# Three tiles in turn for the decay factors and three for the states of the selective scans

## The reference, cut to what matters

```
def step(h, inp):
    u_t, d_t, B_t, C_t = inp
    dA = jnp.exp(d_t[..., None] * A)
    h = dA * h + (d_t * u_t)[..., None] * B_t[:, None, :]
    y = jnp.einsum('bdn,bn->bd', h, C_t)
    return (h, y)
```

## Time and profile before

| | |
|---|---|
| median of 3 runs | 951.99 us (950.78 to 953.58) |
| span of the profiled execution, first to last instruction | 951.3 us |
| DVE busy | 798.0 us, 84% |
| PE busy | 771.3 us, 81% |
| ACT busy | 552.9 us, 58% |
| POOL busy | 513.2 us, 54% |

### The profile page before, as it was taken

The page is one execution under the profiler, slowest core; times in us unless marked ns, Lnnn a source line. Parts: engine busy times, 40 slices in busy tenths (PEclk is TensorE's granted clock), DMA queues, the critical chain, the costliest instruction groups (busy, mean ns, idle before and its releaser), DMA issues. The chain is left out here.

```text
span 951.3 us, 10709 instructions
## 1 busy us (share of the span) xinstructions
PE 771.3 (81%) x3950; PEld 512.7 (54%) x3950; DVE 798.0 (84%) x671; ACT 552.9 (58%) x953; POOL 513.2 (54%) x240
## 2 busy tenths in 40 slices
PE   3999998987666778688799899898766677877895
PEld 2444443444366667678655444344435566866773
DVE  5899886269899898999989978725889999999983
ACT  3664332126758898889477433212484779888932
POOL 2005995020478697778410299901126969867841
PEclk8899999999899899999899999989998999999998
DMA  3000000000535345355200200000033445545521
GB/s 108 1 0 0 0 0 1 0 1 0 166 111 177 130 179 185 127 178 178 67 1 0 67 1 0 0 0 1 1 99 110 156 156 177 190 144 177 160 86 22
DMA packets 33296, 75.03 MB, mean 79 GB/s; under 512 B 15708, under 2 KB 15844, under 8 KB 33248
## 3 DMA queue, kind: packets, MB, share of 16 engines
q1 hardware_dynamic: 31840, 73.09, 23.2%
q0 software_dynamic: 320, 1.05, 0.5%
q10 hardware_dynamic: 1088, 0.26, 0.1%
HBM read 70.71 MB, written 2.62 MB: 77 GB/s over the span
## 5 line engine op out<-in xcount | busy, mean ns | idle before, releaser
L370 POOL TENSOR_TENSOR arena<-arena 128x1024 f32<-128x1024 f32 x127 | 300.7, 2381 | 92.7 <-DVE arena L1705 81.8
L1705 DVE TENSOR_TENSOR_SCAN arena<-arena,ps 128x1024 f32<-128x1024 f32 x128 | 289.4, 2280 | 19.2 <-ACT arena L931 11.4
L931 ACT ACTIVATE arena<-arena 128x128 f32<-128x128 f32 (+3 forms) x408 | 152.4, 448 | 86.2 <-DVE arena L1632 75.3
L931 ACT ACTIVATE arena<-arena,Amat 128x1024 f32<-128x1024 f32 x128 | 146.0, 1145 | 61.1 <-DVE arena L1705 60.4
L618 PE MATMUL ps<-mat,arena 128*128 128x128 f32 x1016 | 136.4, 279 | 3.3 <-POOL arena L370 2.5
L577 PE MATMUL ps<-mat,arena 128*128 128x128 f32 x560 | 79.1, 287 | 73.3 <-DVE arena L1705 58.6
L618 PEld LDWEIGHTS ps<-mat,arena 128*128 128x128 f32 x1016 | 119.0, 145 | 6.0 <-POOL arena L370 3.7
L577 PEld LDWEIGHTS ps<-mat,arena 128*128 128x128 f32 x560 | 63.3, 142 | 90.6 <-DVE arena L1705 74.2
L737 PE MATMUL ps<-arena,mat 128*128 128x512 f32 x240 | 106.3, 592 | 0.0
L931 ACT ACTIVATE arena<-ps 128x1024 f32<-128x1024 f32 (+2 forms) x65 | 56.1, 873 | 82.5 <-PE ps L449 23.6
L480 PE MATMUL ps<-arena,diag 128*128 128x512 f32 x180 | 83.0, 618 | 2.4 <-DVE ps L1543 2.4
(11 more groups left out here) (205 smaller groups left out, 1291.6 us busy)
## 6 DMA issues: line engine op xcount, KB each, us to landing
arena<-c_rows SPq DMA_DIRECT2D x128, 512.0 KB, 4.0
out<-arena SPq DMA_DIRECT2D x28, 64.0 KB, 2.3
xres<-x POOLq DMA_DIRECT2D x4, 256.0 KB, 5.5
xres<-x SPq DMA_DIRECT2D x4, 256.0 KB, 4.1
arena<-arena SPq DMA_DIRECT2D x4, 252.0 KB
convw<-conv_w SPq DMA_DIRECT2D x1, 576.0 KB
c_rows<-ROWS SPq DMA_DIRECT2D x4, 128.0 KB, 1.9
mat<-mats SPq DMA_DIRECT2D x1, 448.0 KB, 3.9
```

Source lines behind the costliest of these rows:

```text
L370: tt(HC[s % 2], HS[s % 2], CB[s % 4], ALU.mult).then_inc(S("hc"), 1)
L931: return nc.scalar.activation(out_, in_, func, bias=bias, scale=scale, accum_out=accum_out)
L1705: nc.vector.tensor_tensor_scan(HS[q], DA[q], PS[q][:, :], 0.0, ALU.mult, ALU.add).then_inc(S("scan"), 1)
```

## The change

The decay factors take three tiles in turn and so do the states; the waits move out by one scan accordingly. The third `DA` tile is laid over the second half of `BCS` and all of `BT` in the second arena, columns that `TB` partly held; `TB` of that arena moves to the first half of `BCS`. The third `HS` tile is a tensor of its own, 4 KB a partition. `PS` and `HC` keep two tiles, `CB` four, and no stream changes its order.

```
-            d["TB"] = d["BCS"][:, L // 2:L]
+            d["TB"] = d["BCS"][:, 0:L // 2] if k else d["BCS"][:, L // 2:L]
+            at = sum(n for _, n in later[:6])
+            d["DA2"] = arena[:, at + L // 2:at + L // 2 + L]
...
-        DA, HS = [[D[0][f"W{2 * m + q}"] for q in range(2)] for m in (0, 2)]
+        DA = [D[0]["W0"], D[0]["W1"], D[1]["DA2"]]
+        HS = [D[0]["W4"], D[0]["W5"], sb("HS2", L)[:, :]]
...
-                tt(HC[s % 2], HS[s % 2], CB[s % 4], ALU.mult).then_inc(S("hc"), 1)
+                tt(HC[s % 2], HS[s % 3], CB[s % 4], ALU.mult).then_inc(S("hc"), 1)
...
-                    j, q = s // D_STATE, s % 2
+                    j, q = s // D_STATE, s % 3
...
-                    if s >= 2:
-                        act.wait_ge(S("scan"), SCANS * h + s - 1)
+                    if s >= 3:
+                        act.wait_ge(S("scan"), SCANS * h + s - 2)
...
-                if s >= 2:
-                    dve.wait_ge(S("hc"), SCANS * h + s - 1)
-                nc.vector.tensor_tensor_scan(HS[q], DA[q], PS[q][:, :], 0.0, ALU.mult, ALU.add).then_inc(S("scan"), 1)
+                if s >= 3:
+                    dve.wait_ge(S("hc"), SCANS * h + s - 2)
+                nc.vector.tensor_tensor_scan(HS[s % 3], DA[s % 3], PS[q][:, :], 0.0, ALU.mult, ALU.add).then_inc(S("scan"), 1)
...
-                tt(half(HC[1], n), half(HS[1], n), half(CB[3], n), ALU.mult).then_inc(S("end_hc"), 1)
+                tt(half(HC[1], n), half(HS[(SCANS - 1) % 3], n), half(CB[3], n), ALU.mult).then_inc(S("end_hc"), 1)
```

## The result

The changed kernel takes 944.7 us in the median of 4 runs (944.05 to 944.92), the kernel before 952.8 us beside it; the ratio is 0.9925 with a 95% interval from 0.9906 to 0.9944. Forecast were 945.4 us (940.5 to 950.5) and faster with a chance of 0.72. The ratio is not the quotient of these two medians, which is 0.9915 and lies in the interval. A second set of runs of the change gave 0.9929 [0.9912, 0.9946].

The account below looks back on a forecast made before the run. DVE was taken to set the pace in both scan stretches, with 15.8 us of waits at scans. Gains of 3.70 us (first half) and 2.92 (second) made 6.6, so 952.0 - 6.6 = 945.4 us, range 940.5 to 950.5.

Parts of the forecast that it names:

- Scans 11, 16, 17: First half: waits put on ACT; 2.2 us gained of 3.91, the 1.40 before scan 11 going whole.
- Scan 21: First half: waited for product 19, would need only product 18, long done; 0.56 us gained.
- Scans 28 and 30: Each half: POOL late by delta_u, but ACT saturated up to decay(30); 0.46 us gained of 0.88.
- Scan 37 and the sum at 38: Pauses of 2.32 and 1.0 us: first tied to scan 34 by two PS tiles, second to PE's out_proj; gain 0.
- Scan 59: Each half: ACT's waits before decay(52) and decay(54) go, the rest is its own work; 0.48 us gained.
- Scans 13 and 17 of the second half: Scan 13 waited for product 11, scan 17 for ACT; 1.57 and 0.41 us gained.
- rival D: Slower: PE sets the pace in steps at TensorE's lower clock, 0.7 us a step; 20 more give 959.4 us; chance 0.06.
- bound of 11.2 us: Most the change could gain: all 15.8 us of DVE's scan waits but the two pauses at scan 37 (4.65).
- rival C: The pauses at scan 37 and the rest go too: 15.8 us less, 936.2 us; chance 0.05.
- Rival A: ACT stays as late as it was; only what the state tiles free goes, 3.05 us: 949.0 us; chance 0.13.
- E: The change doesn't do what it says, some wait comes at the same place: 951.5 to 952 us; chance 0.06.
- rival B: DVE's two-SBUF-input products meet fresh POOL products at shared ports; gain falls to 1.8 us, 950.2 us; chance 0.12.

Follow-up runs that it names:

- orders on before: Kernel before, two tiles each, with PE's turn of the second image's output ahead of step 36's transposes and the layer norm one step later: 950.9 us, 0.9992.
- states alone: Against the kernel before, three state tiles with the new wait, two decay-factor tiles with the old: 949.7 us, 0.9979.
- decay factors alone: Against the kernel before, three decay-factor tiles with the new wait, two state tiles with the old: 948.9 us, 0.9963.
- turn first: Changed kernel with PE's turn of the second image's output ahead of the transposes for step 36, both halves: 945.3 us, 0.9921 to before.
- tiles alone: Against the kernel before, three tiles each for decay factors and states, but the old waits: 951.95 us, 0.9998.
- spread kernel: Changed kernel with turn first, logarithm at step 4, skip and out_proj spread over PE's steps 36 to 38, layer norm two steps later: 942.6 us, 0.9887 to before.
- norm later: Turn first kernel with the first two images' whole layer norm one step later on every engine: 938.8 us, 0.9857 to before.
- spread, eased: Spread kernel with PE's turn of the normed block one step earlier (45) and ACT's last_scale one later (48): 934.9 us, 0.9832 to before.
- both orders: Changed kernel with turn first, layer norm one step later and the logarithm at step 4, without the spreading: 939.3 us, 0.9861 to before.

## Why the prediction was right

Term by term, against the start of each scan in the profile after. The time fell within the range and near its middle. Each ring's share and the pauses before scans 16, 17 and 37 were followed by an experiment of their own.

- *Scans 11, 16, 17*: 2.2 us forecast, 2.16 won by scan 17. The 1.40 went whole, 2.1 of the other 2.5 stayed. Right too was the reason, ACT held by the small matmul and then by its own length: `small_group_var` began and decay(17) ended, counted from scan 0, within 0.1 us of where I had put them, and the logarithm moved away freed the rest. Another 0.33 us came at the gate behind scan 17, which I had at 0. They are not the change's: the gate's wait is also gone in "orders on before", which has two tiles each (last section).
- *Scan 21*: 0.56 forecast, 0.64 won. The third state tile does clear this pause ("states alone"). But the pause stood behind a sum at TensorE's lower clock, which the profile after does not have at that place, and "decay factors alone" won it without the state tile. So that execution would probably have won it in any case: here the forecast had some luck.
- *Scans 28 and 30*: 0.46 forecast in each half; 0.48 and 0.64 won by scan 31, and 0.1 more at scan 45.
- *Scan 37 and the sum at 38*: 0 forecast, 0 won, for the reason given: the turn first shows it.
- *Scan 59*: 0.48 forecast, 0.70 won in the first half and 0.65 in the second.
- *Scans 13 and 17 of the second half*: 1.57 and 0.41 forecast, 1.66 and 0.51 won; 0.11 went again at `delta(3)`.

The mechanism held and the sizes were small: 6.6 us forecast for the scans, 8.1 won. Nearly all of the 1.5 us between comes from four places.

- A closed pause pays more than it shows. Two scans back to back start 2.20 us apart (290.47 and 292.67 above) and yet each is 2.29 us long, as one begins before the other's end is told; a scan behind a pause lacks that. So the 1.40 us before scan 11 were worth 1.47, the 1.57 before scan 13 1.66. Six pauses were closed whole, which makes about 0.5 us.
- On ACT the same holds. Before decay(52) and decay(54) it had waited 0.21 and 0.27 us; with these waits closed the two start 0.31 and 0.36 us earlier behind their predecessors, and that gave scan 59 its 0.7. Both halves: 0.4 us.
- TensorE's clock gave the 0.33 us at the gate. Some 0.15 us at scans 32 and 33 of the second half fit it as well: they are won in every version but the two ("tiles alone", "orders on before") that have a stretch at the lower level near that place, as the kernel before has.
- About 0.1 us was won at scan 45 in each half.

Some readings of mine were poor. The first scans start at 250.1 us and not at 265, so that DVE's mean step there is 214.2 / 64 = 3.35 us and not 3.1, and a step with PE at the low clock would cost 0.45 us and not the 0.7 of rival D. The 15.8 us of waits hold 0.95 us before the first scan of the second half, which stays in every version and which no third tile can free, so that the bound of 11.2 us and the price of rival C were that much too high. And I took the profiled execution to stand 0.7 us under the median. For the later runs span and time of one execution are both given and lie 2.0 us apart (942.9 and 944.92), so the profile of before was of one of the longer executions, about 953.3 us.

Rival A (ACT stays late) and E (nothing changes) fell with the pauses before scans 11 and 13, C with scan 37. Rival D found nothing: the stretches at the lower clock fell from 16 to 12. What I gave for it doesn't hold either: in "orders on before" the same transposes took 1.09 us after the same 1.93 us of idleness. Of rival B the trace shows little: the two `delta(3)` last 2.50 and 2.65 us for 2.44 and 2.50 before, and no third product of this kind was hit. They are longer because they begin earlier beside their product of POOL (0.82 us after its start in place of 0.95 in the second half); they end about 1.1 us after it ends, before the change and after. That is the 0.11 us lost at scan 18 of the second half.

```profile
315.01 2.50 DVE L1687 TENSOR_TENSOR arena<-arena 128x1024 f32<-128x1024 f32 x1
```

The rule of the Trainium skill ("SBUF — State Buffer", Who interferes with whom) that a DVE instruction with one SBUF input does not contend with GpSimd agrees with the scans here: 2.28 us in all versions, whatever POOL did beside them.

## What to carry to other kernels

When a buffer is added to a ring, take each pause singly and ask what its releaser was doing just before: if it was waiting for the ring, the pause goes until the next cause, which is often the length or the order of that engine's own queue, and the profile's releaser need not name it. Slack from a third buffer can also be what makes reordering pay: the same edits of order were worth 3 us in the scans with three tiles and nothing with two, where new pauses took it back. And a wait in an in-order queue should stand where its answer is already there; one instruction too early held ACT for 7 us in the spread kernel and cost 7.7 us of the time.

## What the runs showed of the hardware

The parts outside the scans hold the same instructions in all versions and took from 522.0 to 527.8 us in the profiled executions, more of a difference than most edits here were worth. Cut at the scans, with the mean granted share of TensorE's clock behind each part:

| kernel | before the scans | between them | tail |
|---|---|---|---|
| before | 250.1 (0.952) | 243.4 (0.958) | 32.5 (0.907) |
| the change | 249.3 (0.979) | 243.9 (0.958) | 32.5 (0.914) |
| norm later | 248.7 (0.979) | 242.8 (0.958) | 31.1 (0.950) |
| spread, eased | 249.6 (0.979) | 241.4 (0.965) | 31.1 (0.966) |
| both orders | 248.8 (0.979) | 246.8 (0.938) | 32.2 (0.902) |
| orders on before | 248.0 (0.959) | 243.9 (0.958) | 31.1 (0.958) |

The tail follows the clock: in all thirteen profiles it took 32.2 to 32.5 us at 0.902 to 0.914 and 31.1 us at 0.942 to 0.966. The part between the scans follows it too at its ends, 246.8 us at 0.938 and 241.4 at 0.965, but spreads over 242.8 to 244.1 us at one and the same 0.958. The part before the scans doesn't: its shortest, 248.0 us, came at 0.959, and 249.6 at 0.979. The stretches by windows (us of window, busy time and count of PE, weight loads, DVE, ACT and POOL, granted clock, DMA share, GB/s), first of the eased kernel, then of the one with both orders:

```profile
455.00:697.00 242.00, 212.26 (x666) 105.23 (x665) 188.81 (x187) 107.87 (x131) 89.04 (x43) 0.96 0.05 13
...
902.00:933.00 31.00, 19.52 (x115) 12.41 (x113) 15.57 (x30) 7.47 (x12) 3.79 (x3) 0.97 0.08 18
```

```profile
456.00:702.00 246.00, 217.52 (x656) 107.70 (x655) 188.28 (x186) 106.99 (x131) 87.82 (x43) 0.94 0.04 13
...
908.00:940.00 32.00, 20.41 (x113) 13.24 (x112) 15.17 (x30) 7.47 (x12) 3.79 (x3) 0.90 0.08 17
```

Between the scans PE is busy 5.3 us longer in the second of these, with the work of DVE, ACT and POOL the same within 1.3 us, and the stretch is 5.4 us longer. That stretches at 1.2 GHz in place of 2.4 fell on work of PE for which DVE waits is the plain reading, but no run was made to separate it. Which edit will meet it I could not foretell. Of the 3.1 us that "norm later" won outside the scans 1.4 are in the tail, at 0.950 for 0.914; the other 1.7 came at the same mean clock as in the change, and their cause stays open.

Inside the scans the clock can be caught at one instruction. The gate behind scan 17 waits for a sum of PE. In the kernel before the transposes and this sum took 1.86 and 1.91 us and the gate waited 0.28; in "orders on before", with the same tiles and the same program up to there, they took 1.09 and 1.04 us, after the same 1.93 us of idleness, and the gate did not wait. First the kernel before, then "orders on before":

```profile
315.29 1.91 PE L618 MATMUL ps<-mat,arena 128*128 128x128 f32 x8
317.24 1.22 DVE L1709 TENSOR_TENSOR arena<-ps,arena 128x1024 f32<-128x1024 f32 x1 [0.28 <-PE ps L618]
```

```profile
311.51 1.09 PE L577 MATMUL ps<-mat,arena 128*128 128x128 f32 x8 [1.93 <-DVE arena L1705]
312.44 1.04 PE L618 MATMUL ps<-mat,arena 128*128 128x128 f32 x8
314.75 1.20 DVE L1709 TENSOR_TENSOR arena<-ps,arena 128x1024 f32<-128x1024 f32 x1
```

For comparing versions the scans' stretches were the better measure: they repeated to 0.1 us over two executions of the change, and over the kernel before and "tiles alone". But where a stretch at the lower level moves, as here, a few tenths of a us at one pause are the clock's and not the edit's.
